# Attention loop: another order of work on each engine, norm scaling on GpSimd, gate product in the values' bank

## The reference

```
x = x + attention(ln(x))          # each query sees its 7 x 7 neighbourhood and 16 register keys
t = x as 4608 tokens of 192
n = ln(t)
t = t + sum over the top 2 of 16 experts(weight * expert(n)) + shared(n)
        # experts: silu(n w1) * (n w3) w2, inner 512; shared: the same with inner 1024
        # weights: softmax(n @ gate_w.T), the two largest
```

## Time and profile before

| | |
|---|---|
| median of 3 runs | 1344.66 us (1332.4 to 1348.81) |
| profiled execution, its own time | 1346.43 us |
| its span in the trace | 1344.6 us |
| PE busy | 1163.1 us (86%) |
| DVE / ACT / POOL busy | 503.9 / 406.5 / 391.5 us |
| mean granted TensorE clock | 0.945 |
| exponentials, 432 on ACT | 152.9 us, 436 ns each |
| maxima, 216 on DVE | 118.5 us, 590 ns each |

### The profile page before, as it was taken

The page is one execution under the profiler, slowest core; times in us unless marked ns, Lnnn a source line. Parts: engine busy times, 40 slices in busy tenths (PEclk is TensorE's granted clock), DMA queues, the critical chain, the costliest instruction groups (busy, mean ns, idle before and its releaser), DMA issues. The chain is left out here.

```text
span 1344.6 us, 37382 instructions
## 1 busy us (share of the span) xinstructions
PE 1163.1 (86%) x14806; PEld 954.9 (71%) x14806; DVE 503.9 (37%) x1212; ACT 406.5 (30%) x949; POOL 391.5 (29%) x524
## 2 busy tenths in 40 slices
PE   3899787787787787768999999999999999999990
PEld 2566566666666666645677667679999999999880
DVE  3344555655655655546522212222222222222220
ACT  0244555555555555531111111112222222222110
POOL 3011011111111111100366620004555555555442
PEclk9899888998988998879999989999999999999995
DMA  2352422222222222221113222247888878888754
GB/s 64 120 169 89 117 92 86 79 88 84 81 88 88 78 87 87 79 63 30 30 34 88 70 84 82 78 143 203 213 226 223 219 219 222 214 221 221 199 133 120
DMA packets 111183, 165.18 MB, mean 123 GB/s; under 512 B 14984, under 2 KB 84312, under 8 KB 110824
## 3 DMA queue, kind: packets, MB, share of 16 engines
q1 hardware_dynamic: 91960, 142.68, 34.0%
q0 software_dynamic: 19056, 20.14, 9.2%
HBM read 130.91 MB, written 35.34 MB: 124 GB/s over the span
## 5 line engine op out<-in xcount | busy, mean ns | idle before, releaser
L565 POOL DMA_INDIRECT acc_dram<-ys,lists x87 | 137.6, 1582 | 296.7 <-DVE ys L957 135.1
L618 ACT ACTIVATE probs<-ps,nmax 128x212 f32<-128x212 f32 x432 | 152.9, 436 | 117.4 <-DVE nmax L750 117.4
L750 DVE TENSOR_REDUCE nmax<-ps 128x2 f32<-128x424 f32 x216 | 118.5, 590 | 139.6 <-PE ps L1063 139.2
L950 DVE TENSOR_TENSOR m_h<-m_sg,ps 128x512 f32<-128x512 f32 x87 | 59.8, 687 | 294.8 <-ACT m_sg L664 195.8
L1232 PE MATMUL ps<-xa,w13r 128*128 128x128 f32 x1392 | 169.8, 275 | 0.3 <-ACT xa L658 0.3
L1232 PEld LDWEIGHTS ps<-xa,w13r 128*128 128x128 f32 x1392 | 162.3, 192 | 0.5 <-issue 0.5
L1151 PE MATMUL ps<-c_x,sw13a_sb 64*128 64x384 f32 x768 | 148.6, 498 | 13.1 <-DMA c_x<-xt_dram 4.6
L1076 PE MATMUL ps<-ident_sb,probs 128*98 128x128 f32 x864 | 136.4, 309 | 11.3 <-issue 4.9
L1248 PE MATMUL ps<-w_sb,m_h 128*128 x696 | 136.4, 339 | 0.0
L1076 PEld LDWEIGHTS ps<-ident_sb,probs 128*98 128x98 f32 x864 | 106.6, 147 | 26.5 <-issue 20.2
L651 ACT ACTIVATE s_sg<-ps 128x384 f32<-128x384 f32 x96 | 47.1, 490 | 249.8 <-PE ps L1151 208.7
(11 more groups left out here) (121 smaller groups left out, 1420.4 us busy)
## 6 DMA issues: line engine op xcount, KB each, us to landing
w13r<-in_w13a SPq DMA_DIRECT2D x87, 512.0 KB
w13r<-in_w13b SPq DMA_DIRECT2D x87, 256.0 KB
vst<-v_dram SPq DMA_DIRECT2D x144, 147.0 KB
v_dram<-a_v SPq DMA_DIRECT2D x12, 576.0 KB, 3.3
w_sb<-in_w SPq DMA_DIRECT2D x8, 768.0 KB
xn_dram<-xn SPq DMA_DIRECT2D x36, 128.0 KB
a_x<-in_x SPq DMA_DIRECT2D x12, 288.0 KB, 3.9
x_p<-in_x SPq DMA_DIRECT2D x36, 96.0 KB
```

Of the source, the lines that this page charges most:

```text
L565: nc.gpsimd.indirect_dma_start(acc_dram, bass.IndirectOffsetOnAxis(ap=lists[:, j, 0:1], axis=0), ys[:, j % V8, :], None, compute_op=ALU.ad ...
L618: nc.scalar.activation(probs[:, batch % 2, r, :], ps[:, r, 0:NKEY], ACT.Exp, bias=nmax[:, batch % 2, r:r + 1]).then_inc(b_exp, 1)
L750: nc.vector.tensor_reduce(nmax[:, batch % 2, 2 * half:2 * half + 2], ps[:, 2 * half:2 * half + 2, 0:NKEY], AX.X, ALU.max, negate=True).the ...
L950: nc.vector.tensor_tensor(m_h[:, j % 2, :], m_sg[:, j % 2, :], ps[:, 2 * (j % 2) + 1, :], ALU.mult).then_inc(d_h, 1)
```

## The change

The order of the lists is another one. ScalarE: exponentials, copies of probabilities, and the token copy last and a tile later (of tile t - 3 in the turn k = 2). VectorE: `probsT_out` first, then the closing pieces, the maxima last; `row_stats` moves to the turn k = 1, and the turn without a VectorE copy of probabilities is k = 1 instead of k = 0. The maxima take three instructions (one bank, one bank, two banks) instead of two, and the first two exponentials wait for one bank each. `row_norm` moves from VectorE to GpSimd, behind `normalize_o`; the bias add `stage_tile` moves behind it and is done for the next tile. TensorE: `values` stands ahead of the closing pieces; `token_T` moves to the turn k = 0 of the next tile, `gate` a tile later. The gate product is written to bank 6, columns 384 to 399, so `o_turn`, which reads bank 6, waits for it, and `values` waits for the logits of an earlier tile to be copied. SyncE stores a tile one step later.

```diff
--- before.py
+++ after.py
@@ -309,7 +309,7 @@
 
         def copies_by(batch):
 
-            on_dve = batch + 1 - (batch + 1) // 3
+            on_dve = batch + 1 - (batch + 3) // 3
             return on_dve, 2 * (batch + 1) - on_dve
 
         block = ctx.enter_context(nc.Block())
@@ -413,8 +413,9 @@
             sp.dma_start(sw2_sb[:], sw2).then_inc(c_w, 16)
             for m in range(3, NT):
                 tile_in(m)
-                tile_out(m - 3)
-            for m in range(NT - 3, NT):
+                if m >= 4:
+                    tile_out(m - 4)
+            for m in range(NT - 4, NT):
                 tile_out(m)
 
             sp.wait_ge(b_lg, NT)
@@ -518,13 +519,26 @@
                                             ALU.mult).then_inc(b_on, 1)
 
             pool.wait_ge(s_attn, 16 * ATTN)
+            def row_norm(m):
+                c = m % 3
+                pool.wait_ge(b_pow, m + 1)
+                if m >= 3:
+                    pool.wait_ge(b_xn2st[c], 16 * (m // 3))
+                    pool.wait_ge(b_xTps, m - 2)
+                for lo, hi, at0 in ((0, D, 0), (128, D, D)):
+                    nc.gpsimd.tensor_scalar(xn2[:, c, at0:at0 + hi - lo], x2[:, c, lo:hi], b_mv[:, 0:1],
+                                            b_rs[:, 0:1], ALU.subtract, ALU.mult).then_inc(b_xn2, 1)
+
+            stage_tile(0)
             for m in range(NT + 2):
-                if m < NT:
-                    stage_tile(m)
                 if m >= 2:
                     root(m - 2)
                 if 1 <= m <= NT:
                     normalize_o(m - 1)
+                if m >= 2:
+                    row_norm(m - 2)
+                if m + 1 < NT:
+                    stage_tile(m + 1)
 
 
             pool.wait_ge(r_done, 1)
@@ -612,7 +626,7 @@
 
             def exps(batch):
                 for r in range(4):
-                    act.wait_ge(b_nm, 2 * batch + r // 2 + 1)
+                    act.wait_ge(b_nm, 3 * batch + min(r, 2) + 1)
                     if batch >= 2:
                         act.wait_ge(b_T, 2 * batch - 2)
                     nc.scalar.activation(probs[:, batch % 2, r, :], ps[:, r, 0:NKEY], ACT.Exp,
@@ -630,15 +644,15 @@
                     act.wait_ge(b_xTst[m % 3], 16 * (m // 3))
                 nc.scalar.copy(xn2T[:, m % 3, :, :], ps[0:96, 7, 0:256]).then_inc(b_xT, 1)
 
-            for turn in range(NBATCH + 9):
-                if turn % 3 == 2 and 0 <= turn // 3 - 2 < NT:
-                    xT_out(turn // 3 - 2)
+            for turn in range(NBATCH + 11):
                 if turn < NBATCH:
                     exps(turn)
                 if 1 <= turn <= NBATCH:
-                    if (turn - 1) % 3 == 2:
+                    if (turn - 1) % 3 == 0:
                         probsT_out(turn - 1, 0)
                     probsT_out(turn - 1, 1)
+                if turn % 3 == 2 and 0 <= turn // 3 - 3 < NT:
+                    xT_out(turn // 3 - 3)
 
             act.wait_ge(r_sub, 1)
             nc.scalar.activation(rt[1][:], rt[0][:], ACT.Exp).then_inc(r_exp, 1)
@@ -746,9 +760,8 @@
                 dve.wait_ge(b_S, 8 * batch + 8)
                 if batch >= 2:
                     dve.wait_ge(b_exp, 4 * batch - 4)
-                for half in range(2):
-                    nc.vector.tensor_reduce(nmax[:, batch % 2, 2 * half:2 * half + 2],
-                                            ps[:, 2 * half:2 * half + 2, 0:NKEY], AX.X, ALU.max,
+                for lo, hi in ((0, 1), (1, 2), (2, 4)):
+                    nc.vector.tensor_reduce(nmax[:, batch % 2, lo:hi], ps[:, lo:hi, 0:NKEY], AX.X, ALU.max,
                                             negate=True).then_inc(b_nm, 1)
 
             def probsT_out(batch):
@@ -760,6 +773,8 @@
             def o_turn(m):
 
                 dve.wait_ge(b_V, 12 * m + 12)
+                if m >= 3:
+                    dve.wait_ge(b_gps, m - 2)
                 if m:
                     dve.wait_ge(b_on, 3 * m)
                 nc.vector.transpose(o_raw[:, :, :].rearrange("p h x -> p (h x)"), ps[:, 6, 0:3 * 128]).then_inc(b_oraw, 1)
@@ -782,50 +797,43 @@
                 dve.wait_ge(b_xb, m + 1)
                 if m >= 3:
                     dve.wait_ge(b_x2st[c], 16 * (m // 3))
+                    dve.wait_ge(b_xn2, 2 * (m - 2))
                 nc.vector.tensor_tensor(x2[:, c, :], ps[:, 7, 0:D], xb[:, c, :], ALU.add).then_inc(b_x2, 1)
 
             def row_stats(m):
                 dve.wait_ge(b_x2, m + 1)
+                if m:
+                    dve.wait_ge(b_xn2, 2 * m)
                 step(nc.vector.bn_stats(b_st[:, :], x2[:, m % 3, :]))
                 dve.sem_inc(passed_dve, 1)
                 step(nc.vector.bn_aggr(b_mv[:, :], b_st[:, :]))
                 nc.vector.tensor_scalar(b_ve[:, :], b_mv[:, 1:2], 1e-5, None, ALU.add).then_inc(b_var, 1)
 
-            def row_norm(m):
-                c = m % 3
-                dve.wait_ge(b_pow, m + 1)
-                if m >= 3:
-                    dve.wait_ge(b_xn2st[c], 16 * (m // 3))
-                for lo, hi, at0 in ((0, D, 0), (128, D, D)):
-                    nc.vector.tensor_scalar(xn2[:, c, at0:at0 + hi - lo], x2[:, c, lo:hi], b_mv[:, 0:1],
-                                            b_rs[:, 0:1], ALU.subtract, ALU.mult).then_inc(b_xn2, 1)
-
             def logits_out(m):
                 dve.wait_ge(b_gps, m + 1)
-                nc.vector.tensor_copy(logits[:, m, :], ps[:, 7, 0:E]).then_inc(b_lg, 1)
+                nc.vector.tensor_copy(logits[:, m, :], ps[:, 6, BAND:BAND + E]).then_inc(b_lg, 1)
 
             maxima(0)
             dve.wait_ge(s_wo, 2)
-            for turn in range(NBATCH + 9):
+            for turn in range(NBATCH + 11):
                 t, k = turn // 3, turn % 3
+                if 1 <= turn <= NBATCH and k != 1:
+                    probsT_out(turn - 1)
                 if k == 0 and 0 <= t - 2 < NT:
                     add_x(t - 2)
-                if k == 1 and 0 <= t - 3 < NT:
-                    logits_out(t - 3)
-                if k == 1 and 0 <= t - 1 < NT:
-                    o_turn(t - 1)
-                if 1 <= turn <= NBATCH and (turn - 1) % 3 != 2:
-                    probsT_out(turn - 1)
-                if k == 1 and 0 <= t - 1 < NT:
-                    o_sums(t - 1)
+                if k == 1:
+                    if 0 <= t - 2 < NT:
+                        row_stats(t - 2)
+                    if 0 <= t - 1 < NT:
+                        o_turn(t - 1)
+                    if 0 <= t - 4 < NT:
+                        logits_out(t - 4)
+                    if 0 <= t - 1 < NT:
+                        o_sums(t - 1)
                 if k == 2 and 0 <= t - 1 < NT:
                     o_back(t - 1)
                 if turn + 1 < NBATCH:
                     maxima(turn + 1)
-                if k == 0 and 0 <= t - 2 < NT:
-                    row_stats(t - 2)
-                if k == 1 and 0 <= t - 2 < NT:
-                    row_norm(t - 2)
 
 
             def wide(a):
@@ -1084,6 +1092,8 @@
                 if b == 0:
                     pe.wait_ge(b_vld[m % 3], 64 * (m // 3) + 64)
                     pe.wait_ge(b_oraw, m)
+                    if m >= 4:
+                        pe.wait_ge(b_lg, m - 3)
                 on_dve, on_act = copies_by(batch)
                 pe.wait_ge(b_TcD, on_dve)
                 pe.wait_ge(b_TcA, on_act)
@@ -1100,8 +1110,8 @@
 
             def project(m):
                 pe.wait_ge(b_oT, 2 * m + 2)
-                if m:
-                    pe.wait_ge(b_xT, m)
+                if m >= 2:
+                    pe.wait_ge(b_xT, m - 1)
                 for a in range(2):
                     ins = mm(ps[:, 7, 0:D], oT[:, a, :], wo_sb[:, a, :],
                              start=a == 0, stop=a == 1)
@@ -1109,33 +1119,37 @@
 
             def token_T(m):
                 pe.wait_ge(b_xn2, 2 * m + 2)
-                pe.wait_ge(b_lg, m)
+                pe.wait_ge(b_x2, min(m + 2, NT))
+                if m:
+                    pe.wait_ge(b_xT, m)
                 for k in range(2):
                     ins = tr(ps[0:96, 7, 128 * k:128 * (k + 1)], xn2[:, m % 3, 96 * k:96 * (k + 1)], ident_sb[:, :])
                 ins.then_inc(b_xTps, 1)
 
             def gate(m):
                 pe.wait_ge(b_xT, m + 1)
-                pe.wait_ge(b_x2, min(m + 2, NT))
+                if m:
+                    pe.wait_ge(b_lg, m)
                 for k in range(2):
-                    ins = mm(ps[:, 7, 0:E], xn2T[:, m % 3, k, :], gate_sb[:, k, :], start=k == 0, stop=k == 1)
+                    ins = mm(ps[:, 6, BAND:BAND + E], xn2T[:, m % 3, k, :], gate_sb[:, k, :], start=k == 0, stop=k == 1)
                 ins.then_inc(b_gps, 1)
 
             scores(0)
-            for turn in range(NBATCH + 9):
+            for turn in range(NBATCH + 11):
                 t, k = turn // 3, turn % 3
                 if turn + 1 < NBATCH:
                     scores(turn + 1)
                 if turn < NBATCH:
```

(13 more changed lines are left out.)

## The result

The changed kernel takes 1235.8 us (median of 4 runs, 1222.8 to 1238.9), against 1346.4 for the kernel before in the same comparison (median of 4, 1332.4 to 1348.8): ratio 0.918, 95% interval 0.909 to 0.927. In a second comparison the same two kernels gave 1243.3 against 1337.6, ratio 0.932 (0.925 to 0.939), a gain of 94 us. A ratio leaves out runs more than 1.5% above the fastest of their kernel, so it need not be the quotient of the medians: in experiment 9 it rests on three of six runs, and the medians there give 0.924. The profiled execution of the changed kernel took 1233.5 us, its span is 1231.7.

What follows compares the result with a forecast made beforehand. The attention loop's ScalarE stall and the slower TensorE clock behind it were taken as the bound: 68 us stall plus 26 clock, 2 given back, 92 off 1346.4, gives 1254 us; range 1241 to 1300.

Steps and rivals of the forecast that it cites:

- later stages as before: Feed-forward stages behind the loop, 743.5 us with no line edited, were to keep their time.
- The low bound: Whole kernel: 1242 us, from tiles of 9.54 us with maxima that help.
- Tiles at 9.75 us: Attention loop: three turns sum to 9.65 us, plus 0.1 for unseen joins, against 12.45 us per tile before.
- the ring: Loop: four banks hold one batch, so scores, maxima, exponentials and next scores follow each other; 3.18 us a turn, unchanged.
- The third exponential: Each turn, maxima split in three: it starts when the last maximum is there, 1.29 us, as today; no change.
- The stall: Turn k = 1: ScalarE's token copy, waiting for late transposes, delays exponentials by 2.0 us a tile; 68 us in all.
- The clock: Loop: TensorE, idle in the stall, then runs at the lower level; 0.77 us a tile, 26 us to regain.
- The turn k = 0 at 3.25 us: TensorE's list there, with token transposes and gate, sums to 3.34 us at most, 3.25 with overlaps.
- The list of k = 2: TensorE's scores, transposes, values and projection sum to 3.14 us, under 3.18; the turn takes 3.2 us.
- The new wait for the gate: Rival, k = 1: VectorE's turning of values, then maxima, come late and take part of the gain; about 1298 us, 22%.
- No stall moved: Rival: waiting for logits or GpSimd's normalizing puts a 2 us hole back in each tile; about 1335 us, 7%.
- the clock didn't fall: Rival: the lower clock level stays in the denser loop, tiles of 14.9 us; 1430 us, 4%.

Runs made afterwards that it cites:

- experiment 9: The changed kernel with the projection ahead of the values in TensorE's turn k = 2: 1236.1 us, ratio 0.914 to the kernel before, loop 340.7 us.
- experiment 5: The changed kernel with the maxima in two instructions of two banks again: loop 351.1 us.
- experiment 3: The kernel before with only ScalarE's token copy moved behind its turn's exponentials and copies of probabilities: 1258.1 us, ratio 0.941, loop 371.9 us.
- 7: The kernel before with the token copy last in ScalarE's turn and TensorE's values ahead of the closing pieces: 1251.8 us, ratio 0.933, loop 355.4 us.
- experiment 4: The kernel before with the values product computed twice in the turn k = 1: 1315.3 us, ratio 0.985.
- experiment 8: The changed kernel with the token transposes in TensorE's turn k = 1 instead of k = 0: 1241.3 us, ratio 0.929 to the kernel before, loop 343.8 us.

## Why the prediction was wrong, and where it was right

- **The step that failed is "later stages as before".** The sum hung on one profiled execution and took its 743.5 us behind the loop for the kernel's own. Unchanged code has 722 to 746 us there, and the range had no term for it; it had only the loop's own bounds. Of the 21 us between 1254.5 and the profiled 1233.5, 15.2 are this. The second comparison, 1243.3, lies inside the range, and its gain of 94 us is near the 92 of the forecast; both are the luck of the draw, since the loop and the piece behind it gained 98 to 104. (The low bound, too, is 1 to 2 us off: 34 x (12.45 - 9.54) and 4 for the maxima, taken from 1346.4, leave 1243.5, not 1242.)
- **Tiles at 9.75 us were mis-sized**: (485.2 - 158.7) / 34 = 9.60, with a hiccup that lengthens two of them, 9.47 to 9.69 for nearly all the others; 5 us. The cause is the ring, kept at 3.18 us in all turns, and 0.1 us for joins that didn't show. The third exponential was worked out to start no earlier with three maxima, 1.29 us; in fact the row goes 0.41 and the last ends at 1.97 instead of 2.05. I had allowed that gain for k = 1 alone, and it came in k = 2 too (experiment 5).
- **The stall and its origin in time were right, its size for the copy alone (experiment 3) was not.** The 97 us of loop are made up of 73 (copy, with the clock), 16.5 (values behind the late token transposes, experiments 3 and 7), and 8 to 12 for all the rest of the change: the split, the later tokens, and the bank of the gate. I gave ScalarE's copy the whole 2.0 us; it hid 0.8 us in which TensorE is late by its own list.
- **The clock was right**: forecast 26 us, measured 20 to 22 by experiment 4, in which five stretches at the lower level were left and the added work cost something itself, and a loop at 0.98 or 1.00.
- **The turn k = 0 at 3.25 us** came out at 3.33, and not for the reason given, so that it came close is luck. Its own list isn't what holds it (experiment 8). The list of k = 2, forecast at 3.14 us and under the ring's 3.18, takes 3.27, and the scores at the head of k = 0 start late by it. The pieces' lengths had been read in the old order, transposes 0.91 and projection 0.75; with the values moved between them they take 1.01 and 0.85 (experiment 9 gives the old lengths back with the old order).
- **Costed at nothing and measured at nothing**: normalizing on GpSimd (1.57 us, cover 6.9), one tile more of depth (18.2 us behind the loop against 19.1), SyncE's later stores (TensorE nowhere waits for the windows of values).
- Of the rivals none came. The new wait for the gate is there, 20 times and 4.8 us of VectorE in all, but at most 0.3 us long, and the maxima behind it are as early as elsewhere (a median of 1.08 us after the scores' start). No stall moved, and the clock didn't fall.

## What to carry to other kernels

In a ring of engines, look for the instruction that stands ahead of the ring's own work and whose input is young; moving that one line behind the ring's work brought three quarters of the loop's gain, one more move of the same kind on TensorE most of the rest, and a deeper pipeline, another engine, another bank and a split together 8 to 12 us. The length of a piece read in one order need not hold in another: 0.1 us on each of two pieces was enough to fill a list. A hole on TensorE is paid twice, once as the wait and once as the slower clock behind it, and here most of the second part could be bought back even with useless matmuls (20 to 22 us of loop). When a forecast rests on one execution, profile or time the untouched stages twice before taking their length as fixed: here they moved by more than the error of the part that was thought through.

## What the runs showed of the hardware

- An instruction on GpSimd that subtracts one per-partition scalar and multiplies by another takes 1011 ns for 128x192 and 578 ns for 128x64, in the changed kernel's loop (the rows give busy us in all, then mean ns).

```profile
L529 POOL TENSOR_SCALAR xn<-x,b_mv,b_rs 128x192 f32<-128x192 f32 x34 | 34.4, 1011 | 0.0
...
L529 POOL TENSOR_SCALAR xn<-x,b_mv,b_rs 128x64 f32<-128x64 f32 x33 | 19.1, 578 | 0.0
```

- On VectorE the pair, in the kernel before, took 0.66 to 0.89 us in the 33 tiles in which GpSimd's bias add ran at the same time, and 0.59 and 0.60 in the two with GpSimd idle. That the bias add is the cause was not tested.

```profile
428.67 0.88 DVE L800 TENSOR_SCALAR xn<-x,b_mv,b_rs 128x192 f32<-128x192 f32 x2
...
579.18 0.59 DVE L800 TENSOR_SCALAR xn<-x,b_mv,b_rs 128x192 f32<-128x192 f32 x2
```

- A reduction from PSUM over 212 columns takes 374 ns, over 424 columns 590, in the changed kernel:

```profile
L764 DVE TENSOR_REDUCE nmax<-ps 128x1 f32<-128x212 f32 x216 | 71.8, 374 | 71.7 <-PE ps L1071 70.3
L764 DVE TENSOR_REDUCE nmax<-ps 128x2 f32<-128x424 f32 x108 | 63.7, 590 | 0.0
```

- In two traces TensorE stops once in the middle of a batch of scores, with nothing shown that it waits for. In the kernel of experiment 9 the stop is 1.5 us long, a stretch at the lower clock followed, and the two turns around it took 5.1 and 4.6 us instead of 3.1. The first trace of the changed kernel has a stop of 1.0 us just before 340, with a stretch at the lower clock behind it and turns of 4.3 and 4.8 us. The cause stays open; no run was made for it.

```profile
412.16 0.38 PE L1061 MATMUL ps<-k_T,q_T 32*64 32x196 f32 x1 [1.52 <-issue]
```
